# Hidden-dimension chunks of a mixture-of-experts kernel: 112, 112, 112, 112, 120, 120 rows in place of 115 and 114, and the down weights in two transfers in place of sixteen

## The chip, the cores and the metric

The kernel runs on one NeuronCore of one Trainium2 chip. The metric is the device time of one execution in microseconds (us). Three plain executions were timed, and one more was profiled; all rows below are from the profiled one.

## What is computed

The reference works on x of shape (4, 256, 256) in float32: four sequences of 256 tokens, 1024 tokens in all, of width 256. It is a chain of four residual layers:

```python
x = x + attn_a(layernorm(x), ...)        # layer 0: 16 heads
x = x + ffn(layernorm(x), router_w, Wg, Wu, Wd)   # layer 1
x = x + attn_b(layernorm(x), ...)        # layer 2: 32 query heads, 8 key heads
x = x + ffn(layernorm(x), router_w, Wg, Wu, Wd)   # layer 3, the same weights as layer 1
```

The feed-forward layer is the part that matters here. It has E = 8 experts with a hidden dimension I = 688:

```python
logits = xf @ router_w.T
top_vals, top_idx = jax.lax.top_k(logits, 2)
top_w = jax.nn.softmax(top_vals, axis=-1)
for e in range(8):
    h = silu(xf @ Wg[e].T) * (xf @ Wu[e].T)      # 1024 x 688
    y = h @ Wd[e].T                              # 1024 x 256
    out = out + combine[:, e:e + 1] * y
```

## The kernel before, in words

**Routing.** The kernel computes only the two experts that each token chose. A token's normed row is written ("scattered") into a DRAM tensor `slots_in` (`xs_d`) at a slot that lies in its expert's part, and a second DRAM tensor `row_of_slot` records which output row belongs to the slot. Both are done per sequence ("batch" b = 0 to 3) by GpSimd in `scatter_gpsimd`: four indirect transfers of 128 rows of 1 KB (line 1203; below "row scatters"), then four indirect transfers of 128 single 4-byte words (line 1206; below "word scatters"). Batches 0 and 2 count on the semaphore `scatter0`, batches 1 and 3 on `scatter1`.

**Expert tiles.** There are then 23 tiles of 128 slots (`SLOTS_T`), each belonging to one expert. For a tile, SyncE loads 128 slots (`load_tile`, line 1215), TensorE transposes them (line 1243), multiplies with the gate and up weights in 16 matmuls (line 1256), transposes the 128 x 688 hidden values in six chunks (line 1267, `CH` wide at column offset `CO`), VectorE copies the first four chunks from PSUM to `hT` (line 1320) and ScalarE the last two (line 1300), and TensorE multiplies the six chunks with the down weights in 12 instructions (line 1278). In `experts_tensor` tile i's up matmuls stand between the transposes and the down matmuls of tile i - 1.

**Weights.** All the gate and up weights of the eight experts lie in SBUF in `wgu` (`in_wgu`, 1376 KB for one expert, line 1448), all the down weights in `R1` (`in_wd`). Both are loaded for layer 1 and stay for layer 3, where only experts 6 and 7 of `wgu` are loaded again. Until late in layer 0, `R1` and parts of `wgu` hold attention data, so the weights can't come earlier.

**The down weights** are held in chunks, the hidden row being the partition: chunks 0 to 3 of an expert as 115 partitions of 4 x 256 floats (`in_wd4`), chunks 4 and 5 as 114 partitions of 2 x 256 floats (`in_wd2`), two transfers for each expert. The host lays the arrays out from `CH` and `CO`, so their shapes follow from these (lines 1685 and 1686).

**What sets the order of the work.** The order is written out by hand, each engine has its own instruction stream, and semaphores join them. SyncE's stream around the change is: the placing transfers of batch 3, a wait for the scores of batch 2 and for those placements, the sixteen down-weight transfers (lines 1489 to 1491), a wait for the values product of batch 2, gate and up weights of expert 3, a wait for the last scores of batch 3 (`shifted`, line 1497), gate and up of experts 5, 6 and 7, a wait for the row scatters of batches 0 and 2 (line 1495), gate and up of expert 4, and then `experts_sync`: a wait for all row scatters (lines 1384 and 1385) and the tile loads. TensorE waits for all eight `wgu` loads (line 1327) before it transposes the first tile, and for the down weights (line 1342) after tile 0's up matmuls. VectorE may overwrite the buffer of normed rows for batch 2 only when the row scatters of batch 1, which may still be reading, have landed on `scatter1` (line 326); TensorE's transposes of them (line 349) stand in the middle of its attention work of batch 3.

Of the kernel before, what the change touches and what calls it, by code (L numbers as in the profile page):

```python
# [17 lines left out]
P = 128  # L18
B, S, D = 4, 256, 256
# [17 lines left out]
E, I, TOPK = 8, 688, 2  # L37
IH = I // 2
GU = 2 * I
CH = [115, 115, 115, 115, 114, 114]  # L40
CO = [0, 115, 230, 345, 460, 574]
ROUTED = T * TOPK

SLOTS_T = (ROUTED - E) // P + E
# [41 lines left out]
def build_hybrid(nc, dr, out):  # L86

    ctx = ExitStack()
    with ctx:
        def sb(name, shape, dt):  # L90
            return ctx.enter_context(nc.sbuf_tensor(name, shape, dt))

        def sem(name):
            return ctx.enter_context(nc.semaphore(name))
# [3 lines left out]
        R1 = sb("R1", [P, E * 6 * D], F32)  # L98
        R2 = sb("R2", [P, 6144], F32)
# [12 lines left out]
        masks = sb("masks_sb", [P, 2, 2 * P], BF16)  # L112
        sel = sb("sel_sb", [PARTS * 32, 32], BF16)
        xn = XN[:, :].rearrange("p (t d) -> p t d", t=NT)
        wd = R1[0:CH[0], :]

# [7 lines left out]
        o = 2 * HA * S  # L126
        stage = [R1[:, o + i * 2048:o + (i + 1) * 2048].rearrange("p (n a s) -> p n a s", n=4, a=2) for i in range(2)]
        o = 3 * KD * GU
# [8 lines left out]
        o = 0  # L137
# [30 lines left out]
        o = 0  # L168
# [1 line left out]
        xsT = R2[:, o:o + 512].rearrange("p (n k s) -> p n k s", n=2, k=KD); o += 512  # L170
        sg = R2[:, o:o + I]; o += I
        hh = R2[:, o:o + I]; o += I
        hT = R2[0:CH[0], o:o + 2 * 6 * P].rearrange("p (n c s) -> p n c s", n=2, c=6); o += 2 * 6 * P
        yo = R2[:, o:o + 512].rearrange("p (n d) -> p n d", n=2); o += 512
        assert o <= 6144, o

        o = 0
# [19 lines left out]
        o = 0  # L197
# [30 lines left out]
        BK = [ctx.enter_context(nc.psum_tensor(f"bank{i}", [P, 512], F32)) for i in range(8)]  # L228
# [16 lines left out]
        s_wd = sem("s_wd")  # L245
# [37 lines left out]
        def later(eng, sem, count):  # L283

            if not (isinstance(count, int) and count == 0):
                eng.wait_ge(sem, count)
# [951 lines left out]
        def tile_transpose(l, i, n, p):  # L1238
            s = FF[l]
            nc.tensor.wait_ge(s[f"xs{p}"], 16 * (n + 1))  # L1240
            later(nc.tensor, s["x_e"], i)
            for kk in range(KD):
                last = nc.tensor.transpose(BK[6][:, kk * P:(kk + 1) * P], xs[:, p, kk * P:(kk + 1) * P], ident[:, :])  # L1243
            last.then_inc(s["x_t"], 1)

        def expert_of(i):
            return nc.tensor.value_load(eid[0:1, bass.ds(i, 1)], min_val=0, max_val=E - 1)
# [13 lines left out]
        def tile_hidden(l, i, n, p):  # L1261
            s = FF[l]
            nc.tensor.wait_ge(s["hid"], 2 * i + 2)
            later(nc.tensor, s["hte_v"], i)
            later(nc.tensor, s["hte_s"], i)
            for c in range(6):
                last = nc.tensor.transpose(BK[4 + c // 4][0:CH[c], (c % 4) * P:(c % 4 + 1) * P],  # L1267
                                           hh[:, CO[c]:CO[c] + CH[c]], ident[:, :])
                if c in (3, 5):
                    last.then_inc(s["hid_t"], 1)  # L1270

        def tile_down(l, i, n, p, e):
# [4 lines left out]
            for c in range(6):  # L1277
                last = nc.tensor.matmul(BK[7][:, 0:D], hT[0:CH[c], p, c, :],  # L1278
                                        wd[0:CH[c], bass.ds(e * (6 * D) + c * D, D)], start=c == 0, stop=c == 5)
            last.then_inc(s["down"], 1)  # L1280
# [29 lines left out]
        def tile_vector(l, i, n, p):  # L1310
            s = FF[l]
            v = nc.vector
            for half in range(2):
                v.wait_ge(s["silu"], 2 * i + half + 1)
                v.wait_ge(s["gu"], 4 * i + 2 * half + 2)
                later(v, s["hid_t"], 2 * i)
                v.tensor_tensor(hh[:, half * IH:(half + 1) * IH], sg[:, half * IH:(half + 1) * IH],  # L1317
                                BK[2 * half + 1][:, 0:IH], ALU.mult).then_inc(s["hid"], 1)
            v.wait_ge(s["hid_t"], 2 * i + 1)
            v.tensor_copy(hT[:, p, 0:4, :], BK[4][0:CH[0], :].rearrange("p (c s) -> p c s", c=4)).then_inc(s["hte_v"], 1)  # L1320


        def experts_tensor(l):
            s = FF[l]
            nc.tensor.wait_ge(s["eid"], 1)
            e = expert_of(0)
            nc.tensor.wait_ge(s_wgu, 16 * (E if l == 1 else E + 2))

            def step(i, n, p, nxt=True):


                e, before = expert_of(i), expert_of(i - 1)
                tile_hidden(l, i - 1, n + p - 1, 1 - p)
                if nxt:
                    tile_transpose(l, i + 1, n + p, 1 - p)
                tile_up(l, i, n, p, e)
                tile_down(l, i - 1, n + p - 1, 1 - p, before)

            tile_transpose(l, 0, 0, 0)
            tile_transpose(l, 1, 0, 1)  # L1340
            tile_up(l, 0, 0, 0, e)
            nc.tensor.wait_ge(s_wd, 32 * E)
            step(1, 0, 1)
            step(2, 1, 0)
            with nc.tensor.Fori(1, (SLOTS_T - 3) // 2) as r:
                step(2 * r + 1, r, 1)
                step(2 * r + 2, r + 1, 0)
            step(SLOTS_T - 2, (SLOTS_T - 2) // 2, 1)
            step(SLOTS_T - 1, (SLOTS_T - 1) // 2, 0, nxt=False)
            tile_hidden(l, SLOTS_T - 1, (SLOTS_T - 1) // 2, 0)  # L1350
            tile_down(l, SLOTS_T - 1, (SLOTS_T - 1) // 2, 0, expert_of(SLOTS_T - 1))
# [111 lines left out]
        @block.sync  # L1463
        def _(sp):
            xd = dr["x"].rearrange("(t p) d -> p t d", p=P)
            for t in range(0, NT, 2):
                sp.dma_start(xres[:, t:t + 2, :], xd[:, t:t + 2, :]).then_inc(s_x[t // 2], 16)
            for dst, src in ((ident[:, :], "ident"), (identb[:, :].bitcast(U16), "identb"), (masks[:, :, :].bitcast(U16), "masks"),
                             (sel[:, :].bitcast(U16), "sel"), (rope[:, :, :], "rope_a")):
                sp.dma_start(dst, dr[src]).then_inc(s_const, 16)  # L1470
            for dst, src in ((wdq, "wdq"), (wdkv, "wdkv")):
                sp.dma_start(dst, dr[src]).then_inc(s_wa, 16)
            for dst, src in ((wkr, "wkr"), (wuq, "wuq"), (wuk, "wuk"), (wuv, "wuv"), (wqr, "wqr"), (woa, "woa")):
                sp.dma_start(dst, dr[src]).then_inc(s_wc, 16)
            sp.wait_ge(s_init, INIT)
            for b in range(2):
                place_a_sync(b)
            route_consts_sync(1)
            for e in range(3):
                load_gate_up(e)  # L1480
            sp.dma_start(wob[:, :, :], dr["wob"].rearrange("(k p) n -> p k n", p=P)).then_inc(s_wb, 16)
            for b in range(2, B):
                place_a_sync(b)
            sp.wait_ge(AT[0]["shifted"], (B - 1) * 3 * GA)
            sp.wait_ge(PA["placed_k"], B * PLACED_K)
            sp.wait_ge(AT[0]["placed"], B * PLACED_A)
            sp.wait_ge(s_slots, 16 * 3)
            wdv = R1[:, :].rearrange("p (e m) -> p e m", e=E)
            for e in range(E):
                sp.dma_start(wdv[0:CH[0], e, 0:4 * D], dr["wd4"][e]).then_inc(s_wd, 16)  # L1490
                sp.dma_start(wdv[0:CH[5], e, 4 * D:6 * D], dr["wd2"][e]).then_inc(s_wd, 16)
            sp.wait_ge(AT[0]["pv"], (B - 1) * GA)
            for e in (3, 5, 6, 7, 4):
                if e == 4:
                    sp.wait_ge(FF[1]["scatter0"], 64 * 2)
                if e == 5:
                    sp.wait_ge(AT[0]["shifted"], B * 3 * GA)
                load_gate_up(e)
            experts_sync(1)
            sp.wait_ge(PA["evac_v"], B * len(BY_V))  # L1500
            sp.dma_start(rope[:, :, :], dr["rope_b"]).then_inc(s_const, 16)
            sp.dma_start(ropek, dr["rope_k"]).then_inc(s_const, 16)
            sp.wait_ge(FF[1]["weights"], 1)
            sp.wait_ge(FF[1]["rows"], 16 * TOPK * NT)
            for dst, src in ((wqb, "wqb"), (wkvb, "wkvb")):
                sp.dma_start(dst, dr[src].rearrange("(k p) n -> p k n", p=P)).then_inc(s_wb, 16)
            fetch_sync(1)
            place_b_sync(0)
            place_b_sync(1)
            route_consts_sync(3)  # L1510
            for b in range(2, B):
                place_b_sync(b)
            sp.wait_ge(AT[2]["shifted"], (B - 1) * 3 * GB)
            for e in range(6, E):
                load_gate_up(e)
            experts_sync(3)
            fetch_sync(3)
            for t in range(NT - 4, NT):
                output_sync(t)
            sp.wait_ge(s_out, 16 * NT)  # L1520
# [176 lines left out]
```

## Time and profile before

| what | us |
|---|---|
| plain executions | 978.23, 978.98, 983.63 |
| their median | 978.98 |
| profiled execution | 969.83 |
| its span, first to last instruction | 967.9 |
| expert tiles of layer 1, first tile's transpose to the last down matmul | about 321 to 511 |
| expert tiles of layer 3, the same | about 750 to 944 |

The times in the rows are microseconds from the start of the span. PE is TensorE, DVE VectorE, ACT ScalarE, POOL GpSimd, SPq the queue of SyncE. "DMA share" is the mean busy share of the core's 16 DMA engines; it can exceed 1 where packets of one engine overlap. "To landing" is the time from the issue of a transfer to the arrival of its last byte. The duration of an SPq row is how long the issue itself held up the queue. In tile names R covers `R1` and `R2`.

### The profile page before, as it was taken

How to read it: one execution, taken by the hardware profiler on the slowest of the kernel's cores; microseconds unless marked ns; L12 is line 12 of the kernel's file. 1: busy time of each engine (PE TensorE's matmuls, PEld its weight loads, DVE VectorE, ACT ScalarE, POOL GpSimd, SP SyncE). 2: the span in 40 equal slices, each digit the busy share in tenths (PEclk: the TensorE clock that was granted, in tenths of full speed). 3: DMA queues.
4: the chain of work that ended last, by engine and by line, in shares of the span. 5: the costliest groups of instructions: out<-in, count | busy, mean ns of one | idle time of the engine just before them, and what ended most of it. 6: DMA issues, size and time to landing. Idle time of an engine off the chain costs nothing.

```text
span 967.9 us, 14828 instructions
## 1 busy us (share of the span) xinstructions
PE 792.2 (82%) x5008; PEld 605.3 (63%) x5009; DVE 358.8 (37%) x860; ACT 246.8 (26%) x493; POOL 222.8 (23%) x260
## 2 busy tenths in 40 slices
PE   1999999999830699999992659999982899999990
PEld 1777777777620477777771536777761577777770
DVE  8443453536230122222227466666443122222212
ACT  1102113132310222222223214445551222222221
POOL 8441040523050011111113400003314011111112
PEclk9999999999955899999996879999995899999996
DMA  7953422043399110000203351111302111001004
GB/s 211 390 121 68 186 55 56 22 109 101 118 186 171 43 33 33 33 33 33 71 17 99 98 161 33 33 44 42 140 18 37 30 33 33 33 33 33 27 17 136
DMA packets 47282, 76.65 MB, mean 79 GB/s; under 512 B 9492, under 2 KB 37268, under 8 KB 45372
## 3 DMA queue, kind: packets, MB, share of 16 engines
q1 hardware_dynamic: 35920, 54.36, 22.3%
q0 software_dynamic: 7344, 19.65, 5.3%
q10 hardware_dynamic: 3968, 1.97, 0.7%
q8 instruction: 32, 0.52, 0.3%
q14 instruction: 18, 0.15, 0.1%
HBM read 42.91 MB, written 23.81 MB: 69 GB/s over the span
## 4 chain that ended last, share of the span: by engine, by line
PE 76%; DMA 10%; DVE 8%; issue 2%; POOL 1%; ACT 1%; another core or an unknown queue 0%; SPq 0%; ACTq 0%; POOLq 0%; DVEq 0%
PE bank L1256 22%; PE bank L1278 12%; PE bank L858 9%; PE bank L484 4%; PE bank L439 3%; PE bank L1267 3%; DMA R<-slots_in 3%; PE bank L513 2%; PE bank L495 2%; PE bank L482 2%; PE bank L429 2%; DMA slots_in<-XN,stat 2%; PE bank L553 2%; PE bank L530 2%; DMA PTR<-rows_out 2%
## 5 line engine op out<-in xcount | busy, mean ns | idle before, releaser
L1256 PE MATMUL bank<-wgu,R 128*128 x736 | 223.2, 457 | 0.0
L1256 PEld LDWEIGHTS bank<-wgu,R 128*128 128x128 f32 x736 | 138.0, 193 | 65.1 <-issue 2.1
L1317 DVE TENSOR_TENSOR R<-R,bank 128x344 f32<-128x344 f32 x92 | 47.2, 513 | 230.3 <-PE bank L1256 230.3
L1278 PE MATMUL bank<-R 115*128 (+1 forms) x552 | 127.0, 379 | 1.3 <-DVE R L1320 1.3
L1278 PEld LDWEIGHTS bank<-R 115*128 115x128 f32 (+1 forms) x552 | 104.6, 190 | 22.7 <-issue 1.8
L623 ACT ACTIVATE PTR<-bank 128x512 f32<-128x512 f32 x144 | 83.3, 597 | 89.3 <-PE bank L484 72.3
L1232 POOL DMA_INDIRECT rows_out<-R,XN x46 | 46.2, 1005 | 201.0 <-ACT R L1308 201.0
L1320 DVE COPY R<-bank 115x512 f32<-115x512 f32 x46 | 31.8, 692 | 112.4 <-PE bank L1267 112.4
L1294 ACT ACTIVATE R<-bank 128x344 f32<-128x344 f32 x92 | 42.0, 457 | 118.8 <-PE bank L1256 118.8
L572 DVE TENSOR_REDUCE XN<-bank 128x2 f32<-128x512 f32 x96 | 63.1, 684 | 8.0 <-PE bank L439 8.0
L1243 PE MATMUL bank<-ident_sb,R 128*128 128x128 f32 x92 | 18.7, 287 | 56.3 <-DMA R<-slots_in 55.7
L1225 POOL DMA_DIRECT2D XN<-row_of_slot x46 | 25.4, 552 | 146.7 <-issue 146.7
L1308 ACT ACTIVATE R<-bank 128x256 f32<-128x256 f32 x46 | 17.7, 384 | 152.6 <-PE bank L1278 152.6
L482 PE MATMUL bank<-XN,sel_sb 96*128 96x256 bf16 x192 | 49.6, 275 | 0.0
L593 DVE COPY XN<-bank 128x256 f32<-128x256 f32 x48 | 20.2, 420 | 75.6 <-PE bank L517 72.5
L1243 PEld LDWEIGHTS bank<-ident_sb,R 128*128 128x128 f32 x92 | 11.7, 147 | 57.1 <-DMA wgu<-in_wgu 40.0
L568 DVE TENSOR_REDUCE XN<-bank 128x4 f32<-128x512 f32 x48 | 33.1, 689 | 38.1 <-PE bank L429 37.7
L349 PE MATMUL bank<-ident_sb,XN 128*128 128x128 f32 x40 | 9.4, 385 | 46.0 <-DVE XN L329 46.0
L901 POOL TENSOR_TENSOR R<-wgu 128x256 f32<-128x256 f32 x32 | 23.2, 724 | 101.6 <-DVE wgu L873 101.6
L1203 POOL DMA_INDIRECT slots_in<-R,stat x12 | 11.6, 969 | 144.9 <-DVE stat L1134 142.2
L858 PE MATMUL bank<-xnT,R 128*128 128x256 f32 (+2 forms) x176 | 42.6, 399 | 2.3 <-DVE wgu L873 1.5
L858 PE MATMUL bank<-wgu,R 96*128 96x256 f32 (+1 forms) x176 | 40.7, 384 | 0.8 <-issue 0.8
(159 smaller groups left out, 1285.9 us busy)
## 6 DMA issues: line engine op xcount, KB each, us to landing
wgu<-in_wgu SPq DMA_DIRECT2D x10, 1376.0 KB, 20.7
slots_in<-PTR POOLq DMA_DIRECT2D x1, 9088.0 KB, 24.2
R<-slots_in SPq DMA_DIRECT2D x46, 128.0 KB, 2.0
R<-R SPq DMA_DIRECT2D x32, 128.0 KB, 2.4
wgu<-R SPq DMA_DIRECT2D x32, 128.0 KB, 2.4
PTR<-rows_out SPq DMA_DIRECT2D x16, 256.0 KB, 3.2
R<-in_wd SPq DMA_DIRECT2D x8, 460.0 KB
wgu<-q_parts SPq DMA_DIRECT2D x12, 192.0 KB
```

What stands on the lines that cost most here:

```text
L482: nc.tensor.matmul(bank[i][:, j * S:(j + 1) * S], sel[:, h:h + 1].broadcast_to([PARTS * 32, P]), nT[:, :], start=False, stop=False, skip_g ...
L484: last = nc.tensor.matmul(bank[i][:, j * S:(j + 1) * S], k(h)[:, 0:P], q(h)[:, :], start=False, stop=j == 1, skip_group_check=True)
L568: nc.vector.tensor_reduce(nmax[:, 0, 4 * g:4 * g + 4], bank[0][:, :].rearrange("p (n s) -> p n s", n=4), AX, ALU.max, negate=True).then_in ...
L572: nc.vector.tensor_reduce(nmax[:, 1, 4 * g + 2 * i:4 * g + 2 * i + 2], bank[1 + i][:, :].rearrange("p (n s) -> p n s", n=2), AX, ALU.max, ...
L623: nc.scalar.activation(PT[:, g % 2, i, :], banks(l, g, True)[i][:, :], ACT.Exp, scale=scale).then_inc(s["exps"], 1)
L858: last = nc.tensor.matmul(dst, w, r, start=kk in (0, None), stop=kk in (1, None))
L1232: g.indirect_dma_start(y_d[:, :], bass.IndirectOffsetOnAxis(ap=rows[:, p:p + 1], axis=0), yo[:, p, :], None).then_inc(s[f"ys{p}"], 16)
L1256: last = nc.tensor.matmul(BK[2 * half + gu][:, 0:IH], xsT[:, p, kk, :], wgu[:, bass.ds(e * (KD * GU) + (kk * GU + gu * I + half * IH), IH) ...
L1278: last = nc.tensor.matmul(BK[7][:, 0:D], hT[0:CH[c], p, c, :], wd[0:CH[c], bass.ds(e * (6 * D) + c * D, D)], start=c == 0, stop=c == 5)
L1294: a.activation(sg[:, half * IH:(half + 1) * IH], BK[2 * half][:, 0:IH], ACT.Silu).then_inc(s["silu"], 1)
L1317: v.tensor_tensor(hh[:, half * IH:(half + 1) * IH], sg[:, half * IH:(half + 1) * IH], BK[2 * half + 1][:, 0:IH], ALU.mult).then_inc(s["hid ...
L1320: v.tensor_copy(hT[:, p, 0:4, :], BK[4][0:CH[0], :].rearrange("p (c s) -> p c s", c=4)).then_inc(s["hte_v"], 1)
```

## The change

The chunks become 112 rows four times and 120 rows twice; their sum is still 688. The views `wd` and `hT` are made 120 partitions high, since the last two chunks are now the larger ones, and VectorE's copy of the first four chunks writes 112 partitions of `hT`. The down weights of all eight experts are loaded by two transfers with three-dimensional patterns (partition, expert, row), and TensorE's wait for them counts 32 in place of 256. Nothing else changes; the number of matmuls, copies and transposes for a tile is the same.

```diff
-CH = [115, 115, 115, 115, 114, 114]
-CO = [0, 115, 230, 345, 460, 574]
+CH = [112, 112, 112, 112, 120, 120]
+CO = [0, 112, 224, 336, 448, 568]
...
-        wd = R1[0:CH[0], :]
+        wd = R1[0:CH[5], :]
...
-        hT = R2[0:CH[0], o:o + 2 * 6 * P].rearrange("p (n c s) -> p n c s", n=2, c=6); o += 2 * 6 * P
+        hT = R2[0:CH[5], o:o + 2 * 6 * P].rearrange("p (n c s) -> p n c s", n=2, c=6); o += 2 * 6 * P
...
-            v.tensor_copy(hT[:, p, 0:4, :], BK[4][0:CH[0], :].rearrange("p (c s) -> p c s", c=4)).then_inc(s["hte_v"], 1)
+            v.tensor_copy(hT[0:CH[0], p, 0:4, :], BK[4][0:CH[0], :].rearrange("p (c s) -> p c s", c=4)).then_inc(s["hte_v"], 1)
...
-            nc.tensor.wait_ge(s_wd, 32 * E)
+            nc.tensor.wait_ge(s_wd, 32)
...
-            for e in range(E):
-                sp.dma_start(wdv[0:CH[0], e, 0:4 * D], dr["wd4"][e]).then_inc(s_wd, 16)
-                sp.dma_start(wdv[0:CH[5], e, 4 * D:6 * D], dr["wd2"][e]).then_inc(s_wd, 16)
+            sp.dma_start(wdv[0:CH[0], :, 0:4 * D], dr["wd4"].rearrange("e p m -> p e m")).then_inc(s_wd, 16)
+            sp.dma_start(wdv[0:CH[5], :, 4 * D:6 * D], dr["wd2"].rearrange("e p m -> p e m")).then_inc(s_wd, 16)
```

## Rows read from the trace of the kernel before

**Rows 1.** Page: the span, and PE's busy tenths in 40 slices.

```profile
span 967.9 us, 14828 instructions
PE   1999999999830699999992659999982899999990
```

**Rows 2.** Chain of work, layer 1: start us, duration us, what; 200 to 330.

```profile
230.81 11.98 DMA slots_in<-wgu,stat
...
285.75 14.93 DMA slots_in<-XN,stat
300.91 19.68 DMA R<-slots_in
320.72 0.67 PE bank L1243 x2
...
329.90 4.63 PE bank L1256 x16
```

**Rows 3.** Chain of work, the same places in layer 3.

```profile
742.02 2.41 DMA slots_in<-XN,stat
...
745.22 8.22 DMA R<-slots_in
...
762.43 4.63 PE bank L1256 x16
```

**Rows 4.** Waits, 290 to 370: engine, line, releaser, us in total, times, longest.

```profile
PEld bank L1243 <- DMA wgu<-in_wgu: 40.0, 1, 40.0
```

**Rows 5.** SyncE's queue by time (start us, us, line); first down-weight issue: 220.50.

```profile
226.82 7.79 SPq L1490 DMA_DIRECT2D R<-in_wd  x1
...
258.05 17.84 SPq L1448 DMA_DIRECT2D wgu<-in_wgu  x5
...
275.52 0.37 SPq L1448 DMA_DIRECT2D wgu<-in_wgu  x1
```

**Rows 6.** Busy time by stretch; the last two columns are DMA share and GB/s.

```profile
100.00:102.00 2.00, 2.00 (x14) 1.44 (x13) 0.00 (x0) 0.88 (x2) 0.00 (x0) 1.00 1.01 418
...
250.00:252.00 2.00, 2.00 (x14) 1.54 (x15) 0.17 (x1) 0.60 (x1) 0.00 (x0) 1.00 0.32 130
...
275.00:280.00 5.00, 2.53 (x12) 2.03 (x10) 1.46 (x12) 2.09 (x3) 0.00 (x0) 0.50 1.26 126
...
300.00:305.00 5.00, 0.00 (x0) 0.00 (x0) 0.00 (x0) 0.00 (x0) 0.00 (x0) 0.50 0.97 47
```

**Rows 7.** DMA issues by landing time (last number), issued at 172.25, 177.3, 267.7, 275.5, 694.5.

```profile
slots_in<-wgu,stat POOLq DMA_INDIRECT x1, 2.4
...
row_of_slot<-wb,stat POOLq DMA_INDIRECT x2, 12.8
...
slots_in<-wgu,stat POOLq DMA_INDIRECT x1, 7.8
...
wgu<-in_wgu SPq DMA_DIRECT2D x1, 1376.0 KB, 44.7
...
slots_in<-R,stat POOLq DMA_INDIRECT x1, 10.8
```

**Rows 8.** DVE and PE in order of time; L495 is batch 3's last scores.

```profile
242.92 0.73 DVE L329 TENSOR_SCALAR wgu<-xres,stat 128x256 f32<-128x256 f32 x2 [1.99 <-DMA slots_in<-wgu,stat]
...
243.71 0.66 PE L349 MATMUL bank<-ident_sb,wgu 128*128 128x128 f32 x4 [0.47 <-DVE wgu L329]
...
258.72 0.44 PE L495 MATMUL bank<-wgu 96*128 96x128 f32 x2
```

**Rows 9.** Groups by form, 322 to 510: busy us, mean ns of one, idle before.

```profile
L1278 PE MATMUL bank<-R 115*128 x184 | 43.6, 379 | 0.7 <-DVE R L1320 0.7
...
L1278 PE MATMUL bank<-R 114*128 x88 | 22.6, 379 | 0.0
...
L1267 PEld LDWEIGHTS bank<-ident_sb,R 128*115 128x115 f32 x92 | 13.2, 179 | 2.6 <-DVE R L1317 1.2
...
L1267 PEld LDWEIGHTS bank<-ident_sb,R 128*114 128x114 f32 x46 | 5.6, 134 | 0.0
```

## The prediction

> **What bounds the kernel now.** The page's slices come first: TensorE is busy in nine tenths or more of most slices, and in layer 1 it falls to 0 in the thirteenth, which is 290 to 315 us [rows 1]. That hole is the place to look at, since a kernel bound by TensorE gains little elsewhere. The chain of waits says what fills it: the last row scatter of batch 3, issued at 285.75, takes 14.93 us, the load of a tile's slots behind it 19.68 us, and only at 320.72 are there transposes again [rows 2]. The list of waits adds a second cause that ends at the same moment: TensorE's weight load waited 40.0 us for gate and up weights [rows 4]; the last of these, expert 4, was issued at 275.52 and landed 44.7 us later, at 320.2 [rows 5, 7]. So it isn't one slow transfer: everything on the DMA engines is late together.
>
> Why, the stretches show. When three gate and up transfers run alone, the DMA share is 1.01 at 418 GB/s; while the down weights run, at 250, it is 0.32 at 130 GB/s [rows 6]. 0.32 of 16 engines is 5.1 engines, and 130 / 418 is 0.31: the down-weight transfers use five engines at full speed and leave eleven idle. Their bytes are 8 experts x 688 x 256 x 4 = 5.64 MB, so at 130 GB/s they take 43.4 us. They also block SyncE, one of whose issues stalls for 7.79 us, and the gate and up weights behind them start at 258.05 [rows 5]. Once those are queued they need all 16 engines, but five still have the backlog, and they set the landing.
>
> The Trainium skill (DMA: Bandwidth & Descriptors, "Why a DMA increments its semaphore by 16 and not by 1") says that a transfer from SyncE uses the largest count up to 16 that divides the size of the slowest dimension on both sides. By that rule 115 rows get 5 engines, 114 get 6, 112 get 16 and 120 get 15; the trace agrees for the old shapes with its share of 0.32, and no row here shows 112 or 120.
>
> Layer 3 is the control. It has the same end of routing and the same first tiles, with no weights in flight: the last row scatter takes 2.41 us and the tile load 8.22 [rows 3]. From that scatter's issue to the up matmuls of the second tile it is 762.43 - 742.02 = 20.41 us, in layer 1 329.90 - 285.75 = 44.15 us [rows 2, 3]. The difference, 23.7 us, is the weights' whole price at this place.
>
> **The change part by part.** *The down-weight transfer itself.* The nearest row for a transfer on all engines is the 418 GB/s one: 5.64 MB take 13.5 us in place of 43.4, from about 220.5 to 234 if nothing disturbs them. The other bound is 130 GB/s, if the new shapes are not spread better. I take 13.5, as the old share is so exactly a divisor's. What matters is only that it ends before 259, when the last scores of batch 3 release experts 5, 6 and 7 [rows 8]; even eight engines (209 GB/s, 27 us) would do that.
>
> *The same skill page* ("Where 436 GB/s comes from") gives about 358 GB/s as one core's limit for loads from HBM. The 418 GB/s here is above it, so the measurement decides; by 358 the transfer would take 15.8 us and the forecast would stay.
>
> *SyncE's queue.* Sixteen issues become two. In place of 37.5 us (220.50 to 258.05) [rows 5] SyncE needs a few at most, issues expert 3 at once, and reaches the wait for the last scores early. Experts 5 to 7 are then issued at about 259 to 260 (before: up to 275.5, expert 4 last), and 4.23 MB at 418 GB/s land by about 270.
>
> *Expert 4* waits for the row scatters of batch 2. The last is issued at 267.7 and landed after 7.8 us [rows 7], that is at 275.5. In the changed kernel it meets a burst on 16 engines; the nearest row is batch 1 in layer 3, where two gate and up loads were in flight: 10.8 us [rows 7]. So expert 4 goes at 275.5 to 278.5. Its 1.41 MB need 3.4 us at 418 GB/s, but they run beside batch 2's word scatters: the last two of these took 12.8 us to land even undisturbed [rows 7], and beside them all queues together moved 126 GB/s at 275 to 280 [rows 6]. At that rate it is 11.2 us. Bounds for the landing are 279 and 290; I take 288. Batch 3's word scatters, issued right after 287, bring the next slow stretch (47 GB/s at 300 to 305) [rows 6]; expert 4 comes before it.
>
> *The start of the expert tiles.* With no weights left it follows layer 3, 23.7 us earlier. I take off 2.5 us, since expert 4's tail lies beside batch 3's row scatters: bound 0 if it is gone by 282, and 2.4 + 8.2 us more for both transfers at worst, short of the old 14.9 and 19.7.
>
> *Batch 1's row scatters.* This is the cover to be checked. They are issued at 227 to 230.81 in the middle of the new burst, and normed rows of batch 2 wait for them. Before, the last took 11.98 us, VectorE waited 1.99 us for it and TensorE then 0.47 us [rows 2, 8]. So landing sooner gives 0.5 us at most, and landing later costs in full. Under a burst the nearest row is 10.8 us [rows 7], about even; the burst here is longer (7 MB with expert 3 against 2.8), and word scatters follow at once. I take 1.0 us lost, bounds 0.5 gained and 4 lost.
>
> *The chunks in the expert loop.* 46 tiles, no instruction more or less. The down matmuls take 379 ns with 115 rows and with 114 alike; the transposes' weight loads took 179 ns for 115 columns and 134 for 114, but beside matmuls [rows 9]. Copies with 112 or 120 partitions have the same length in columns. I take nothing. Bounds: six loads by 45 ns by 46 tiles are 12 us in either direction if they didn't overlap.
>
> *What is late next.* The rest of the kernel hangs on the end of layer 1's tiles, a loop in which TensorE hardly waits (0.7 us in 184 matmuls) [rows 9], and layer 2's transfers are issued after it. So what is gained at 330 is kept to the end.
>
> The sum: 23.7 - 2.5 - 1.0 + 0 = 20.2 us, call it 20.5 as batch 1 may cost less. The profiled execution would go from 969.83 to about 949.3. The median before is 978.98, 9.2 us above the profiled one; nothing says that the part that changes differs, so the forecast is 978.98 - 20.5 = 958.5 us.
>
> **The rivals.** (1) *Stalls given back.* The burst and the word scatters hit each other harder than in the old kernel: batch 1's row scatter lands 4 us late, and expert 4 slips into the stretch of batch 3's word scatters and lands at about 305 in place of 288. Tiles then start at about 306, 14 us earlier than at 320.7, less 4: a gain of 10, 969 us. For it speaks that even 10.8 us was seen with 2.8 MB in flight; against it, that the queues hold fewer bytes from 270 on. (2) *A larger gain.* The plain executions may have a longer queue than the profiled one, as they are longer. The cap is the whole transfer's saving, 43.4 - 13.5 = 29.9 us: 949 us. (3) *The change doesn't do what it says.* If three-dimensional patterns, or these sizes, still land on five engines, all stays: 979 us. For it speaks only that no row shows the new shape. (4) *Slower.* The expert loop pays for the new chunk sizes: 18 instructions a tile (line 1267 six, line 1278 twelve) by 46 tiles are 828. It cancels the gain from 25 ns each, and 31 ns each give 979 - 20.5 + 25.7 = 984 us. The 45 ns between the two weight loads [rows 9] say that such a thing exists; that matmuls of 114 and 115 rows are equal speaks against it, and that the loads lie beside other work.
>
> By the same skill section's rule, engines for 112 and 120 rows are 16 and 15 and rival 3 is out; I leave it a chance by the missing row alone.
>
> **How the numbers follow.** Forecast (gain 15 to 27 us) 0.65; rival 1 (8 to 15) 0.18; rival 2 (over 27) 0.05; rival 3 0.07; rival 4 0.05. The likeliest time is 958.5, its own range 952 to 964. The range that should hold 8 in 10 reaches over rival 1 and the spread of the plain executions: 949 to 970. About 0.5% (4.9 us) is what a measurement of this kernel can tell from no change. Faster by more: 0.65 + 0.18 + 0.05 = 0.88; within: 0.07; slower by more: 0.05.
>
> **What would show each step.** Right: in the stretches from 222 to 234 a DMA share near 1 and about 400 GB/s; two short issues in SyncE's queue and expert 3 before 230; experts 5 to 7 issued at about 260; expert 4 landing before 292; the second tile's up matmuls at 305 to 311; the loop's 379 ns a down matmul unchanged. Wrong: a share of 0.32 again (rival 3); VectorE's wait at line 329 of more than 5 us, or expert 4 landing after 300 (rival 1); longer transposes or down matmuls (rival 4). A gain in layer 1 that is smaller at the end of the span would mean that a wait in layer 2 or 3 that I took for covered isn't.

## The result, and the profile after

| what | before, us | changed, us |
|---|---|---|
| median of the four timed executions | 978.61 | 962.25 |
| their span of values | 974.09 to 983.63 | 961.6 to 962.69 |
| profiled execution | 969.83 | 962.69 |

The medians differ by 16.4 us, or 1.7%, where 20.5 (978.98 to 958.5) were forecast. The ratio of the means, with the profiled execution of before counted in, is 0.985, with a 95% interval of 0.981 to 0.989. Two further comparisons on other chips gave 0.985 (0.982 to 0.988) and 0.986 (0.980 to 0.992).

The page of the changed kernel, to be read against [rows 1]: the hole in TensorE's slices is still there, and shorter (a 0 and a 6 have become a 1 and a 9).

```profile
span 960.9 us, 14814 instructions
PE   1989999999931999999974379999981999999990
```

SyncE's queue of the changed kernel (start us, us), against [rows 5]. The two down-weight transfers take 1 us to issue, and expert 3's gate and up weights go out at 227.38, 31 us sooner. The x5 of that line counts on to expert 4, whose own issue is the last line: 277.94, 2.4 us later than before.

```profile
222.34 0.35 SPq L1489 DMA_DIRECT2D R<-in_wd  x1
222.73 0.61 SPq L1490 DMA_DIRECT2D R<-in_wd  x1
...
227.38 50.94 SPq L1448 DMA_DIRECT2D wgu<-in_wgu  x5
...
277.94 0.37 SPq L1448 DMA_DIRECT2D wgu<-in_wgu  x1
```

Busy time by stretch, against [rows 6]; the last two columns are DMA share and GB/s. The first rows are the down weights: all 16 engines busy, but at 233 to 281 GB/s. The last three are the stretch that matters: the engines are called busy and move next to nothing.

```profile
224.00:226.00 2.00, 2.00 (x15) 1.73 (x14) 1.86 (x14) 0.00 (x0) 0.00 (x0) 1.00 0.97 281
226.00:228.00 2.00, 2.00 (x31) 1.27 (x30) 1.84 (x5) 0.00 (x0) 0.00 (x0) 1.00 1.03 233
...
275.00:280.00 5.00, 2.50 (x12) 2.20 (x12) 1.52 (x11) 1.99 (x3) 0.00 (x0) 0.67 0.35 16
280.00:285.00 5.00, 0.75 (x23) 0.69 (x23) 3.65 (x18) 0.09 (x1) 1.81 (x2) 0.50 0.98 64
285.00:290.00 5.00, 0.00 (x0) 0.00 (x0) 1.13 (x8) 0.00 (x0) 3.78 (x5) 0.50 0.82 51
```

The chain of work, against [rows 2]. The tile load behind the scatter fell from 19.68 to 5.60 us, but the last row scatter of batch 3 takes 15.01 us, as much as before (14.93), where the same scatter in layer 3 took 2.41 [rows 3].

```profile
286.70 15.01 DMA slots_in<-XN,stat
301.94 5.60 DMA R<-slots_in
...
318.35 4.63 PE bank L1256 x16
```

Issues by landing time, against [rows 7]: the last row scatter of batch 1 (issued at 232.66), expert 4's gate and up weights (277.94) and the last row scatter of batch 3 (286.70).

```profile
slots_in<-wgu,stat POOLq DMA_INDIRECT x1, 6.4
...
wgu<-in_wgu SPq DMA_DIRECT2D x1, 1376.0 KB, 15.8
...
slots_in<-XN,stat POOLq DMA_INDIRECT x1, 15.0
```

One measure carries the comparisons below: from the issue of batch 3's last row scatter to the start of the second tile's up matmuls. It is free of whatever an execution lost or won earlier. Its values come from the instructions in order of time, so they are 0.1 to 0.2 us below those that the prediction took from the chain.

| kernel (profiled execution) | layer 1, us | layer 3, us |
|---|---|---|
| before | 44.0 | 20.2 |
| changed | 31.5 | 20.4 |
| changed, two more chips | 31.3, 31.0 | 19.9, 21.1 |

So the place where the change works gained 12.5 to 13 us of a possible 23.7. The medians differ by more, 15 to 16 us in the three comparisons. That the profiled executions differ by only 7.1 us comes from the other side: between layer 1's second tile and layer 3's last row scatter the profiled execution of before took 412.3 us, and the three of the changed kernel 416.8, 420.6 and 418.5. A kernel with the times of before, shown next (`old2`), took 419.5 there. The stretch varies by 8 us between executions, and the one of before was a lucky one. One piece of it in the changed kernel is the row below, of its chain between attention steps of layer 2. The chain of before has no such row there, and that of `old2` has one of 6.03 us, so it doesn't come with the change; of what VectorE waited for, the profile shows no more:

```profile
655.35 5.17 another core or an unknown queue
```

### The profile page after: what moved, and what is told of

It is laid out like the page before. It is cut to its first block, busy times and chain, and to the rows that moved or that the text cites. A ratio compares the mean times of both kernels' runs of the same rounds, so it can differ in the third digit from the quotient of the medians.

```text
span 960.9 us, 14814 instructions
## 1 busy us (share of the span) xinstructions
PE 795.1 (83%) x5008; PEld 606.4 (63%) x5009; DVE 358.5 (37%) x860; ACT 246.7 (26%) x493; POOL 223.0 (23%) x260
## 4 chain that ended last, share of the span: by engine, by line
PE 75%; DVE 8%; DMA 8%; SPq 3%; issue 2%; ACT 1%; POOL 1%; another core or an unknown queue 1%; ACTq 0%; POOLq 0%; DVEq 0%
PE bank L1256 23%; PE bank L1278 12%; PE bank L858 6%; PE bank L484 4%; PE bank L439 4%; PE bank L1267 3%; PE bank L495 2%; PE bank L513 2%; PE bank L429 2%; PE bank L482 2%; DMA slots_in<-XN,stat 2%; PE bank L553 2%; PE bank L530 2%; DMA PTR<-rows_out 2%; SPq L913 2%
## 5 line engine op out<-in xcount | busy, mean ns | idle before, releaser
L1278 PE MATMUL bank<-R 112*128 (+1 forms) x552 | 127.0, 379 | 1.3 <-DVE R L1320 1.3
L1278 PEld LDWEIGHTS bank<-R 112*128 112x128 f32 (+1 forms) x552 | 104.7, 190 | 22.6 <-issue 1.8
L1320 DVE COPY R<-bank 112x512 f32<-112x512 f32 x46 | 31.8, 691 | 112.4 <-PE bank L1267 112.4
L593 DVE COPY XN<-bank 128x256 f32<-128x256 f32 x48 | 20.2, 420 | 78.3 <-PE bank L517 68.8
L1267 PE MATMUL bank<-ident_sb,R 128*112 128x128 f32 (+1 forms) x276 | 37.8, 273 | 1.4 <-DVE R L1317 1.4
## 6 DMA issues: line engine op xcount, KB each, us to landing
wgu<-in_wgu SPq DMA_DIRECT2D x10, 1376.0 KB, 11.1
```

## The experiments

**The two parts apart.** The theory was that the chunk sizes alone bring the gain, by the number of DMA engines that a transfer uses; the rival that it is the number of transfers, by SyncE's time. All on one chip, with the changed kernel beside them.

> The changed kernel once more, beside the parts of it on the same chip. All theories: a gain of 14 to 18 us on the kernel before, as measured the first time (962.25 against 978.61).

Measured: 963.04 us against 978.18, ratio 0.985 (0.982 to 0.988).

New sizes, sixteen transfers (against the changed kernel, as are all edits below but the next):

```diff
-            nc.tensor.wait_ge(s_wd, 32)
+            nc.tensor.wait_ge(s_wd, 32 * E)
...
-            sp.dma_start(wdv[0:CH[0], :, 0:4 * D], dr["wd4"].rearrange("e p m -> p e m")).then_inc(s_wd, 16)
-            sp.dma_start(wdv[0:CH[5], :, 4 * D:6 * D], dr["wd2"].rearrange("e p m -> p e m")).then_inc(s_wd, 16)
+            for e in range(E):
+                sp.dma_start(wdv[0:CH[0], e, 0:4 * D], dr["wd4"][e]).then_inc(s_wd, 16)
+                sp.dma_start(wdv[0:CH[5], e, 4 * D:6 * D], dr["wd2"][e]).then_inc(s_wd, 16)
```

> Chunk sizes of the change, but the sixteen transfers of the kernel before. Theory (the spread over the DMA engines by the chunk size brings the gain): as the changed kernel within 3 us, DMA share near 1 from the first down-weight transfer on. Rival (fewer transfers bring it, through SyncE's issue time): as the kernel before, within 3 us. By the way: in the changed kernel the 4 KB packets took a median of 310 ns at 226 to 230 us against 159 ns before; if the three-dimensional order causes this, packets here take 159 ns and the down weights end some 5 us sooner, with no effect on the time, since experts 5 to 7 are released only at 260.

Measured: 962.80 us, ratio 0.985 (0.982 to 0.988), the same as the whole change. The 4 KB packets of the down weights took some 250 ns in the trace's DMA records, where they took 159 ns in the kernel before, so the three-dimensional order is not what slows them.

Old sizes, two transfers (`old2`, against the kernel before):

```diff
-            nc.tensor.wait_ge(s_wd, 32 * E)
+            nc.tensor.wait_ge(s_wd, 32)
...
-            for e in range(E):
-                sp.dma_start(wdv[0:CH[0], e, 0:4 * D], dr["wd4"][e]).then_inc(s_wd, 16)
-                sp.dma_start(wdv[0:CH[5], e, 4 * D:6 * D], dr["wd2"][e]).then_inc(s_wd, 16)
+            sp.dma_start(wdv[0:CH[0], :, 0:4 * D], dr["wd4"].rearrange("e p m -> p e m")).then_inc(s_wd, 16)
+            sp.dma_start(wdv[0:CH[5], :, 4 * D:6 * D], dr["wd2"].rearrange("e p m -> p e m")).then_inc(s_wd, 16)
```

> Chunk sizes of the kernel before, two transfers in place of sixteen. Theory: as the kernel before within 3 us, since five and six engines carry the down weights as before; DMA share 0.32 again. Rival (fewer transfers bring the gain): as the changed kernel.

Measured: 979.52 us, ratio 1.001 (0.998 to 1.003). Two transfers don't even free SyncE: the second issue holds its queue for 27.51 us, while the stretches show 131 GB/s at a share of 0.32 to 0.34. That fits a queue which takes no more until its few busy engines have drained; no run here shows how much it holds.

```profile
219.54 0.35 SPq L1489 DMA_DIRECT2D R<-in_wd  x1
219.94 27.51 SPq L1490 DMA_DIRECT2D R<-in_wd  x1
247.49 26.68 SPq L1448 DMA_DIRECT2D wgu<-in_wgu  x4
```

The first theory holds: the gain comes from the chunk sizes, and the merging of the transfers is worth nothing that these runs can tell.

**Where the other 11 us stayed.** In the changed kernel batch 2's four word scatters are issued at 270 to 274, and from 275 to 290 hardly anything moves. Expert 4's load (15.8 us) and batch 3's row scatters (9.6 to 15.0 us) lie in this stretch. The first test moves the word scatters of batch 2 (`rows` and `words` say which of its two kinds of scatter a call issues; both are new arguments):

```diff
-            scatter_gpsimd(1, B - 2)
-            scatter_gpsimd(1, B - 1)
+            scatter_gpsimd(1, B - 2, words=False)
+            scatter_gpsimd(1, B - 1, words=False)
+            scatter_gpsimd(1, B - 2, rows=False)
+            scatter_gpsimd(1, B - 1, rows=False)
```

> The changed kernel with one thing moved: GpSimd issues the word scatters of batch 2 behind the row scatters of batch 3 in layer 1. Theory (word scatters in flight hold up the load of expert 4 and the row scatters of batch 3, which took 15.8 and 15.0 us in the changed kernel): expert 4 lands in 4 to 6 us, the last row scatter of batch 3 in 2.4 to 4, the first tile starts 8 to 12 us earlier, the time falls by 4 to 12 us (part may be given back, as eight word scatters now stand together and the first output rows wait for them). Rival (the load of expert 4 alone holds up the row scatters): no change, row scatter of batch 3 again at 12 us or more.

Measured: 956.76 us, 6.3 less than the changed kernel on the same chip. Three of the four executions lie at 956.6 to 956.8, against 960.7 to 965.1; the fourth, 963.75, lies among the latter, so the interval, 0.977 to 0.986, is wide and overlaps that of the changed kernel. The trace has to carry this step. Its landing times: expert 4, the last row scatter of batch 3, and then the load of the third tile, which now meets eight word scatters together:

```profile
wgu<-in_wgu SPq DMA_DIRECT2D x1, 1376.0 KB, 5.7
...
slots_in<-XN,stat POOLq DMA_INDIRECT x1, 2.4
...
R<-slots_in SPq DMA_DIRECT2D x1, 128.0 KB, 15.2
```

The measure fell from 31.3 to 24.4 us. So word scatters in flight are a cause of expert 4's slow load. Of the row scatters' delay they are not enough of one: in layer 3 they stand before the same row scatters at the same distance, and the last of those lands in 2.41 us [rows 3]. Nor does this kernel show what the load does to them, since it landed at 277.6, 3 us before the first of them was issued (280.54). The next kernels take the load away and leave the word scatters. Batch 2's normed rows are moved out of expert 4's place into `wob`, the buffer of layer 2's output weights (whose own load goes behind layer 1's tile loads), and expert 4 needn't wait for them:

```diff
-        xn_a = room(o, 2 * D).rearrange("p (t d) -> p t d", t=2); o += 2 * D
+        xn_a = wob[:, :, :]
...
-            sp.dma_start(wob[:, :, :], dr["wob"].rearrange("(k p) n -> p k n", p=P)).then_inc(s_wb, 16)
...
-            for e in (3, 5, 6, 7, 4):
-                if e == 4:
-                    sp.wait_ge(FF[1]["scatter0"], 64 * 2)
+            for e in (3, 4, 5, 6, 7):
...
+            sp.dma_start(wob[:, :, :], dr["wob"].rearrange("(k p) n -> p k n", p=P)).then_inc(s_wb, 16)
```

> The changed kernel with expert 4's gate and up weights freed of the wait for batch 2's row scatters: the normed rows that lay in their place lie in the buffer of layer 2's output weights, whose load moves behind layer 1's tile loads, and expert 4 is loaded with experts 3, 5, 6 and 7. All word scatters stand where they stood. Theory (word scatters in flight slow every other transfer to a crawl, and the gain that is missing is expert 4's load and batch 3's row scatters lying in batch 2's): the last row scatter of batch 3 lands in 2.4 to 4 us as in layer 3, the first tile starts 8 to 12 us earlier than in the changed kernel, 951 to 956 us. Rival (batch 3's row scatters are held by batch 2's word scatters alone): they land in 10 us or more, 961 us or above.

Its control has the moved rows and the moved `wob` load alone, with the order and the wait of the changed kernel:

> Control: the normed rows lie in the buffer of layer 2's output weights and that load is moved, but expert 4 is loaded last and waits as in the changed kernel. All theories: as the changed kernel, 960 to 965 us; a gain here would mean that the place of the rows, not expert 4's load, is what counts.

Measured: 948.70 us for the one, ratio 0.974 (0.969 to 0.979), and 957.21 for the control, ratio 0.982 (0.977 to 0.987). All four values of the one (948.1 to 949.4) lie below all four of the control (954.7 to 958.4). Both lie below what was expected (951 to 956, and 960 to 965); the kernel before lies at 974.02 on this chip too, 4 us lower than on the others, the changed kernel was not run here, and the control's ratio overlaps its ratio elsewhere, so nothing is made of it. The measure is 20.2 us against 30.4, the whole of what was missing: layer 3's is 20.5. Landing of the last row scatter of batch 3 in the control, then the same and the first tile's load with expert 4 freed:

```profile
slots_in<-XN,stat POOLq DMA_INDIRECT x1, 16.0
```

```profile
slots_in<-XN,stat POOLq DMA_INDIRECT x1, 2.4
R<-slots_in SPq DMA_DIRECT2D x1, 128.0 KB, 8.3
```

So a load of 1.4 MB among word scatters crawls (15.8 us in the changed kernel, 19.0 in the control, 5.7 without them), and where the row scatters meet both, all four take 9.3 to 16.0 us. Beside word scatters alone (expert 4 freed) the four take 5.2, 4.1, 3.1 and 2.4 us. Beside a load alone no kernel has batch 3's; batch 1's in the changed kernel, in the middle of the weights and ahead of their own word scatters, take 6.4 to 7.2. The two together cost more than either.

The last row scatter has a further part that no run separates. In the changed kernel the first three land 10.4, 9.6 and 10.1 us after their issue, by 295.5, and the last at 301.7, though between 295 and 300 nothing moves:

```profile
295.00:300.00 5.00, 0.00 (x0) 0.00 (x0) 0.00 (x0) 0.00 (x0) 0.00 (x0) 0.50 0.00 0
```

What stands right behind it is batch 3's own word scatters. Batch 1 of the kernel before has the same step, 3.6, 3.8 and 3.6 us and then 11.98. That some 6 of the 15 us come from these word scatters is likely, and not shown.

Both moves together:

> The same, and batch 2's word scatters moved behind batch 3's row scatters as in the run before with that move. Theory: with expert 4 out of the way the move has nothing left to gain, and eight word scatters together delay the first tiles' loads (15.2 and 13.1 us in the run before): slower than the kernel with expert 4 freed alone by 1 to 5 us.

Measured: 951.14 us, ratio 0.974 (0.968 to 0.981), with one execution of four at 943.97. The measure is 20.0 us, as with expert 4 freed alone; the median is 2.4 us above. The sign is as expected, but it can't be told from none.

**One step further.** With expert 4 freed, the tile loads (8.3 us against some 2 us for later ones in the changed kernel) are what is late, beside batch 3's own word scatters. GpSimd holds these back until the first two tiles have landed (`behind` is a new argument, given for batch 3 in layer 1 alone):

```diff
+            if behind:
+                nc.gpsimd.wait_ge(s["xs0"], 16)
+                nc.gpsimd.wait_ge(s["xs1"], 16)
             for t, at, mine in both:
                 nc.gpsimd.indirect_dma_start(rows_d[l][:, :],
```

> Expert 4 freed, and GpSimd issues batch 3's word scatters of layer 1 only after the first two tile loads have landed. Theory: the two tile loads take 2 to 3 us instead of 5 to 8, the tiles start another 3 to 6 us earlier, of which the third tile's load, now in the word scatters, may give back some: 947 to 953 us. Rival (what is gained is given back in full by the third tile's load and the late first output rows): as with expert 4 freed alone, within 2 us.

Measured: 943.08 us, ratio 0.969 (0.964 to 0.974), 5.6 below the kernel without it, on the same chip. GpSimd's queue shows the price: a wait of 5.00 us ahead of the word scatters, and the first output rows are stored at 312.84, some 4 us later than ScalarE has them ready. TensorE's loop, 8.10 us a tile, doesn't notice.

```profile
291.32 0.97 POOL L1209 DMA_INDIRECT row_of_slot<-wb,stat  x1 [5.00 <-DMA R<-slots_in]
...
310.30 0.60 POOL L1228 DMA_DIRECT2D XN<-row_of_slot  x1 [14.19 <-issue]
...
312.84 1.00 POOL L1235 DMA_INDIRECT rows_out<-R,XN  x1 [0.83 <-DMA XN<-row_of_slot]
```

The same in layer 3 as well, on a third chip with the changed kernel beside it:

> The changed kernel on the chip of the next two, as their base: all theories 1.2 to 1.8% below the kernel before.

> Expert 4 freed and batch 3's word scatters put behind the first two tile loads in layer 1, and now in layer 3 too. Theory: in layer 3 the last row scatter and the tile loads meet no word scatter of batch 3, the load takes 2 to 4 us instead of 5 to 8, and the time falls by a further 3 to 6 us; against the kernel before 3.4 to 4.2% faster. Rival (given back by the third tile's load): as with layer 1 alone, 3.1%.

Measured: the changed kernel 964.00 us, ratio 0.986 (0.980 to 0.992); the new one 942.06, ratio 0.961 (0.955 to 0.967). That is 38 us below the kernel before on this chip, against 16 for the change. Layer 3's tile load falls from 8.22 us [rows 3] to 2.09 in the chain, and its measure from 18.8 us in the kernel without this step (20.2 in the kernel before) to 14.2. How much of it reaches the end can't be told from the times: the two kernels ran on different chips (943.08 and 942.06 us), and their ratios' intervals touch.

```profile
719.99 2.41 DMA slots_in<-XN,stat
722.62 2.09 DMA R<-slots_in
```

| profiled execution | layer 1, us | layer 3, us |
|---|---|---|
| new sizes, sixteen transfers | 31.7 | 24.0 |
| old sizes, two transfers | 45.8 | 21.0 |
| batch 2's word scatters late | 24.4 | 20.2 |
| normed rows moved (control) | 30.4 | 19.8 |
| expert 4 freed | 20.2 | 20.5 |
| and batch 2's word scatters late | 20.0 | 20.8 |
| expert 4 freed, batch 3's word scatters behind two tile loads | 14.9 | 18.8 |
| the same in layer 3 too | 15.0 | 14.2 |

Layer 3's column shows how far one execution's value can be trusted: no row but the last changes anything there, and it holds 18.8 to 21.0 and once 24.0. In layer 1 the changed kernel's three values and that of the sixteen transfers lie within 31.0 to 31.7.

**Why 16 engines gave 250 GB/s and not 418.** The host pads the down weights to 128 partitions, and the two transfers carry all of them:

```diff
-            sp.dma_start(wdv[0:CH[0], :, 0:4 * D], dr["wd4"].rearrange("e p m -> p e m")).then_inc(s_wd, 16)
-            sp.dma_start(wdv[0:CH[5], :, 4 * D:6 * D], dr["wd2"].rearrange("e p m -> p e m")).then_inc(s_wd, 16)
+            sp.dma_start(wdv[:, :, 0:4 * D], dr["wd4"].rearrange("e p m -> p e m")).then_inc(s_wd, 16)
+            sp.dma_start(wdv[:, :, 4 * D:6 * D], dr["wd2"].rearrange("e p m -> p e m")).then_inc(s_wd, 16)
...
+    for n in ("wd4", "wd2"):
+        arrays[n] = np.pad(arrays[n], ((0, 0), (0, P - arrays[n].shape[1]), (0, 0)))
```

> The changed kernel with the down weights padded by the host to 128 partitions (rows 112 to 127 and 120 to 127 are zeros that nothing reads), 11.6% to 14% more bytes (6.29 MB in place of 5.64). Question: why the 4 KB packets of the down weights, 159 ns each on five engines, take 210 to 310 ns on 16. Theory (two engines meet where the 112 rows of a transfer aren't cut at the same partitions as 128 rows are): packets take 159 ns, rate above 380 GB/s, the 4 KB packets end sooner although there are more of them. Rival (the DRAM side, or SyncE's descriptor generation): packets stay at 210 to 310 ns. The time of the kernel stays within 3 us either way.

Measured: 403 and 406 GB/s in stretches that answer to the 281 and 233 above, and the 4 KB packets back at 159 ns in the trace's DMA records. The padding changes the arrays' layout in DRAM as well as the partitions written, and the run doesn't tell which of the two counts. Its one execution took 960.9 us, so the faster rate buys nothing that it can tell. The reason is in the landing times: the first transfer lands after 15.1 us, the second, which is still in flight when batch 1's word scatters are issued (232.18 to 236.00), after 37.2 us, at 258.2, no sooner than without the padding; and experts 5 to 7 are not released before about 260.

```profile
224.00:226.00 2.00, 2.00 (x29) 1.24 (x28) 1.87 (x5) 0.00 (x0) 0.00 (x0) 1.00 1.03 403
226.00:228.00 2.00, 2.00 (x16) 1.79 (x15) 1.41 (x7) 0.00 (x0) 0.94 (x1) 1.00 1.00 406
```

```profile
R<-in_wd SPq DMA_DIRECT2D x1, 4096.0 KB, 15.1
R<-in_wd SPq DMA_DIRECT2D x1, 2048.0 KB, 37.2
```

## Why the prediction was right, and what it had wrong

**The bound and its cause: right.** A share of 0.32 read as five engines of 16 was the key. The parts alone show it: the sizes carry the gain, the merging none. The prediction put SyncE's freed queue beside this as a second benefit; the two kernels show that the number of issues didn't block the queue: with the new sizes all sixteen are out 8.7 us after the first, and with the old sizes two take 28. The Trainium skill's rule for the number of engines (DMA: Bandwidth & Descriptors, "Why a DMA increments its semaphore by 16 and not by 1") gives 16 and 15 for these sizes, and the share near 1 agrees.

**The down-weight transfer: right in kind, wrong in size.** The share was 0.96 to 1.09 from 224 to 240, but at first at 233 to 281 GB/s, where 418 was taken from the nearest row, one of a 128-partition transfer. The larger miss came later. Batch 1's four word scatters were issued at 233.93 to 237.75, and from 244 to 256 all queues together moved 56 to 95 GB/s:

```profile
244.00:246.00 2.00, 2.00 (x18) 1.83 (x17) 0.00 (x0) 1.86 (x4) 0.00 (x0) 1.00 1.30 95
...
250.00:252.00 2.00, 2.00 (x26) 1.66 (x15) 0.60 (x2) 0.10 (x1) 0.00 (x0) 1.00 0.70 56
```

By the trace's DMA records the last packet of the down weights ended at 258.4 and not at 234, and expert 3's weights landed 35.6 us after their issue, at 263.0. The condition that the prediction set, an end before 259, was met by less than 1 us: that part was luck. It priced word scatters beside expert 4's load and not beside this one, though batch 1's stand in the middle of it.

**Experts 5 to 7 and the issue of expert 4: right.** They were issued at 260.35 to 261.29 (forecast 259 to 260), and expert 4 at 277.94 (forecast 275.5 to 278.5). Experts 5 to 7 moved until about 274, not 270.

**Batch 1's row scatters: the sign was wrong.** One us was taken as lost, from a row of 10.8 us. They landed in 6.4 us in the burst (before: 11.98), VectorE no longer waited for them, and TensorE's transposes came 0.6 us sooner, seen from the scatters' issue: 16.1 us after batch 1's first one against 16.7. The prediction had put the most that an earlier landing could gain at 0.5 us. It had read the row of 10.8 as the price of a burst; a longer burst cost 6.4, so the burst alone isn't the price of that row, and what else was stays open.

**The step that failed** is "I take off 2.5 us, since expert 4's tail lies beside batch 3's row scatters". That place cost 31.5 - 20.4 = 11.1 us in place of 2.5, more than the worst bound given with it (2.4 + 8.2 us). The mechanism had been named (word scatters hold up what runs beside them, 126 GB/s at 275 to 280), and two sizes in it were too small. Expert 4 was given 126 GB/s there; but that was what all queues moved together, with the packets of experts 5 to 7 and of the down weights in flight too. Alone among the word scatters it got 16 to 64 GB/s and landed at 293.7, outside the bounds of 279 to 290. And the row scatters behind it were priced as beside a tail, while they took 15.01 us, all of the old 14.93: this part of the old delay had been ascribed to the weights, and the kernels with expert 4 freed show that it belonged to the word scatters and expert 4 together, which the change didn't move. Rival 1 described this kind of loss (a gain of 10 us in place of 20.5), by expert 4 slipping into batch 3's word scatters and landing at 305. It did reach into them (they were issued from 287.97 on, and it landed at 293.7), but the crawl was there before them, from 278 on.

**The second tile's up matmuls** were forecast for 305 to 311 and started at 318.19. One part of this is not waiting for transfers: the first tile's 16 up matmuls took 7.04 us in place of 5.50. TensorE had been idle since 282; its granted clock stood at 0.50, the lower level of 1.2 GHz, until 310 and at 0.57 over 310 to 315.

**Rival 3** (nothing happens) and **rival 4** (a slower expert loop) fell. The loop's groups, to be read against [rows 9], are the same within 1 ns where they bound; the weight loads of 115 columns, 179 ns, have become 133 for 112:

```profile
L1278 PE MATMUL bank<-R 112*128 x184 | 43.6, 380 | 0.7 <-DVE R L1320 0.7
...
L1278 PE MATMUL bank<-R 120*128 x92 | 23.7, 379 | 0.0
...
L1267 PEld LDWEIGHTS bank<-ident_sb,R 128*112 128x112 f32 x92 | 11.1, 133 | 3.6 <-DVE R L1317 1.2
```

**The sum**: 20.5 us were forecast. By these places it should have been 12.5 + 0.6 = 13.1; the medians moved by 16.4, 15.1 and 16.0. The rest, 2 to 3 us, is not explained: it is within what the stretch after layer 1's first tiles varies by (412 to 421 us), and the 12.5 hangs on one execution of before. With `old2`, whose times are those of before, in its place the measure gained 45.8 - 31.3 = 14.5 us on one chip. The forecast came as near as it did partly because of these 2 to 3 us.

## What to carry to other kernels

Divide the DMA share by one engine's part of 16 before anything else: a share that stands at a plain fraction during a large load (0.32 is five of 16) pointed here at a partition count without a large divisor, and 688 rows cut as 112 and 120 in place of 115 and 114 were worth 1.5%, whatever the number of transfers. When a control stage shows what a place costs undisturbed, ask which of the transfers in flight the control lacks, and also which it shares: here the shared ones (4-byte scatters) cost the row scatters little alone, and 11 us together with one 1.4 MB load. Transfers of single words that nobody needs soon go behind those that somebody waits for; that, and one load freed of a buffer's wait, were worth more than the change.

## What the runs showed of the hardware that was not expected

- A transfer of 112 partitions that kept the DMA share near 1 moved 233 to 281 GB/s, and padded to 128 partitions 403 to 406, from the same place in the kernel. The Trainium skill (SBUF — State Buffer, "Door 1: The DMA port swizzle (why `[64,N]` ≈ `[32,N]`)") says that groups of 4 partitions share a port and that a port serves 8 partitions; if each of 16 engines takes seven neighbouring partitions of 112, engines meet on ports. The runs agree with that, and don't show the ports themselves.
- Of four word scatters, 2 KB in all, the last two took 12.8 us to land alone [rows 7]. Twice in the changed kernel, after four of them had been issued beside weights, all queues together moved next to nothing for 12 to 15 us: 56 to 95 GB/s from 244 to 256 and 16 to 64 GB/s from 275 to 290. What in the memory path causes it, no run here tells.
- The second of the two down-weight issues held SyncE's queue for 27.51 us with 114 rows (DMA share 0.32 to 0.34), and for 0.61 us with 120 rows (share near 1).
